# Attention with a causal mask on one core: the next head's maxima are dealt out over the steps by another table

## The reference

```
attn = jnp.einsum('bhqd,bhkd->bhqk', q, k) * SCALE
attn = jnp.where(causal[None, None], attn, -jnp.inf)
probs = jax.nn.softmax(attn, axis=-1)
out = jnp.einsum('bhqk,bhkd->bhqd', probs, v)
```

## Time and profile before

| | |
|---|---|
| median of three executions | 1719.4 us |
| the profiled execution | 1721.68 us |
| its span, first to last instruction | 1719.9 us |
| what lies outside the span | 1.8 us |
| granted TensorE clock, mean over the span | 0.988 of full |
| PE, DVE, ACT, POOL busy | 97%, 68%, 64%, 53% |

### The profile page before, as it was taken

How to read it: one execution, slowest core, us unless ns; L and a number is a source line. 1 busy time by engine, 2 the same in 40 slices (tenths; PEclk the granted TensorE clock), 3 DMA queues, 4 the chain that set the end, 5 groups by cost and what they waited for, 6 DMA issues and landing times.

```text
span 1719.9 us, 30467 instructions
## 1 busy us (share of the span) xinstructions
PE 1660.3 (97%) x9262; PEld 1369.7 (80%) x9262; DVE 1161.7 (68%) x2377; ACT 1104.9 (64%) x1684; POOL 906.1 (53%) x764
## 2 busy tenths in 40 slices
PE   7999999999999999999986999999999999999996
PEld 7987677767767776776665999999999999999992
DVE  6437777777777777778697676665665566556544
ACT  3222788787878887887686566666665565556544
POOL 2321888878788888882764433434334343343422
PEclk9999999999999999999997999999999999999998
DMA  7676211111111111112664897897987887788776
GB/s 241 188 220 196 62 50 50 49 49 49 49 49 49 49 49 49 49 49 74 232 229 128 287 269 225 245 274 208 281 237 201 224 265 217 208 249 239 192 190 217
DMA packets 103715, 276.87 MB, mean 161 GB/s; under 512 B 19833, under 2 KB 37625, under 8 KB 93625
## 3 DMA queue, kind: packets, MB, share of 16 engines
q1 hardware_dynamic: 78169, 213.29, 38.0%
q0 software_dynamic: 25440, 62.27, 17.4%
HBM read 194.75 MB, written 63.72 MB: 150 GB/s over the span
## 4 chain that ended last, share of the span: by engine, by line
PE 87%; DVE 6%; issue 2%; DMA 2%; ACT 2%; POOL 1%; SPq 0%; DVEq 0%; ACTq 0%; POOLq 0%
PE p_prj L91 26%; PE a_op L883 11%; PE a_mp L842 8%; PE a_sp L901 7%; PE p_at_ps L91 7%; PE p_logit_ps L91 7%; PE e_qp L91 5%; PE a_op L874 5%; PE p_ht_ps L2057 3%; PE e_vp L91 2%; PE p_at_ps L2080 2%; DVE part_max L759 2%; PE a_sp L905 1%; PE a_shared L860 1%; PE a_mp L845 1%
## 5 line engine op out<-in xcount | busy, mean ns | idle before, releaser
L709 POOL TENSOR_TENSOR prob_lo<-prob,prob_hi 128x1024 fp32r<-128x1024 f32 x211 | 451.5, 2157 | 141.6 <-DVE prob_hi L788 132.6
L759 DVE TENSOR_REDUCE part_max<-a_mp 128x1 f32<-128x512 f32 (+2 forms) x600 | 359.5, 610 | 70.5 <-PE a_mp L842 40.4
L1446 POOL DMA_INDIRECT acc_rows<-m_y_out,m_row_ids x108 | 176.1, 1631 | 410.7 <-ACT m_y_out L1615 385.9
L744 ACT ACTIVATE prob<-a_sp 128x1024 f32<-128x1024 f32 x320 | 293.6, 930 | 64.4 <-PE a_sp L905 34.9
L91 PE MATMUL p_prj<-m_w_hi,m_ht_hi 128*128 128x352 f32 x888 | 297.5, 335 | 1.8 <-DVE m_ht_lo L1855 1.4
L91 PE MATMUL p_prj<-m_w_lo,m_ht_hi 128*128 128x352 f32 x888 | 288.0, 324 | 0.0
L91 PE MATMUL p_prj<-m_w_hi,m_ht_lo 128*128 128x352 f32 x888 | 287.0, 323 | 0.0
L1879 DVE TENSOR_TENSOR m_w_lo<-m_w_raw,m_w_hi 128x704 fp32r<-128x704 f32 (+1 forms) x357 | 270.7, 797 | 22.8 <-ACT m_w_hi L1621 22.4
L1621 ACT ACTIVATE m_w_hi<-m_w_raw 128x704 fp32r<-128x704 f32 (+1 forms) x357 | 229.0, 713 | 17.5 <-PE p_prj L91 16.8
L1865 DVE TENSOR_TENSOR m_at_lo<-p_at_ps,m_at_hi 128x384 fp32r<-128x384 f32 x111 | 61.8, 557 | 252.0 <-ACT m_at_hi L1607 252.0
L731 ACT ACTIVATE prob_hi<-prob 128x1024 fp32r<-128x1024 f32 x216 | 203.2, 941 | 6.8
(11 more groups left out here) (314 smaller groups left out, 3336.0 us busy)
## 6 DMA issues: line engine op xcount, KB each, us to landing
m_w_raw<-wexp SPq DMA_DIRECT2D x51, 1408.0 KB
m_w_raw<-wexp SPq DMA_DIRECT2D x51, 768.0 KB
qk_parts<-rows SPq DMA_DIRECT2D x64, 256.0 KB, 3.2
multi<-qk_parts SPq DMA_DIRECT2D x42, 256.0 KB, 5.0
acc_rows<-p_zeros SPq DMA_DIRECT2D x2, 4352.0 KB, 18.8
v_head<-v_all SPq DMA_DIRECT2D x16, 520.0 KB, 3.0
k_stack<-qk_parts SPq DMA_DIRECT2D x21, 256.0 KB, 4.1
q_stack<-qk_parts SPq DMA_DIRECT2D x21, 256.0 KB, 6.2
```

The lines of the kernel that those rows point to most:

```text
L709: nc.gpsimd.tensor_tensor(prob_lo[:, t % RING, :, c0:NB], prob[:, t % RING, :, c0:NB], f32(prob_hi[:, t % RING, :, c0:NB]), ALU.subtract). ...
L744: nc.scalar.activation(prob[:, t % RING, :, c0:NB], sp_[:, t % 2, :, c0:NB], ACT.Exp, scale=SCALE).then_inc(prob_ready, 1)
L759: nc.vector.reduce_max(part_max[:, qb, kb:kb + 1], mp[:, n % 2, 0:width], AX_X).then_inc(piece_done, 1)
L1446: nc.gpsimd.indirect_dma_start(acc_dram[sum_of(t)], bass.IndirectOffsetOnAxis(ap=row_id(t), axis=0), y_out[:, t % 4, :], None, compute_op= ...
```

## The change

One table has other numbers, with the same sum of 40. No instruction is added or removed.

```
-PIECES_AT = (0, 0, 0, 0, 0, 3, 4, 3, 4, 2, 1, 2, 1, 3, 3, 3, 3, 3, 3, 2)
+PIECES_AT = (0, 0, 0, 0, 0, 3, 3, 3, 3, 3, 2, 3, 2, 3, 3, 3, 3, 2, 2, 2)
```

## The result

Over nine executions the changed kernel took 1726.65 us in the median (1724.26 to 1729.43), the kernel before, on the same chips, 1722.88 us (1718.43 to 1723.72). The ratio is 1.0029 with a 95% interval of 1.0019 to 1.0039: slower by 5.0 us (3.3 to 6.7); the two medians alone are 3.8 us apart. The forecast was +3.6 us. It was put as a median of 1723.0 us because the kernel before then had 1719.4 us from three executions; on the 1722.88 us of nine, the same +3.6 gives 1726.5. The interval lies around the bound of 0.3% set beforehand, so the runs say "slower", but not on which side of that bound.

What follows compares the result with a forecast made beforehand. PE, 97% busy, bounds the kernel; its waits for DVE cost 1.6 us per head. Terms -0.46 - 0.40 + 0.21 + 1.00 - 0.09 = +0.26 per head, +3.6 us over 14 heads: median 1723.0 us, range 1715 to 1729.

Steps and rivals of the forecast that it cites:

- Steps 6 and 8: PE no longer waits for piece 6 or back-to-back pieces 12 and 13: 0.46 and 0.40 us saved per head.
- Step 9: Three pieces between half-wide products: PE waits for piece 12's bank and restarts once, 0.21 us added per head.
- 10 to 12: Steps 10 to 12 get one piece more each, 0.24 us of PE work each, with nothing waiting.
- Step 13: Its first piece, 22, waits 0.90 us behind tile 10's subtraction, plus 0.10 restart: 1.00 us added per head; delay ends there.
- 14: Step 14: pieces 23 and 24 come late enough that step 13's delay ends before them; no stall added.
- 15: Step 15: piece 30 waits 0.34 us plus 0.10 restart, against 0.53 before: 0.09 us saved per head.
- 16 to 19: Steps 16 to 19 have two or three pieces with full products between; 0 us of stall change.
- The meeting of DVE and POOL: DVE asks for tile 10 with 0.81 us of POOL's tile 11 left, and pays 0.67 us.
- The slower rival: DVE stays late past step 13, so pieces 26, 28 and 30 wait: +0.56 us per head, 1727.2 us; chance 0.20.
- Only the gains come: Tile 10's subtraction gets ahead of POOL's tile 11 and takes 1.22 us: -0.4 per head, 1713.7 us; chance 0.12.
- the subtraction costs what it did: Tile 10's subtraction on DVE still takes 1.58 us: -0.05 us per head, 1718.7 us; chance 0.16.

Runs made afterwards that it cites:

- experiment 1: Steps 5 to 9 as in the change, later ones as in the kernel before, but step 10 has two pieces instead of one; 1715.03 us, ratio 0.9961 to before.
- experiment 5: Changed kernel, but in step 11 DVE takes tile 10's subtraction ahead of the third piece; 1722.68 us, ratio 1.0005 to the kernel before.
- experiment 6: Table of experiment 1 with one piece moved from step 9 to step 12; 1709.28 us, ratio 0.9931 to the kernel before.
- experiment 2: Steps 5 to 9 as in the kernel before, later ones as changed, but step 16 has two pieces instead of three; 1737.25 us, ratio 1.0090 to before.
- experiment 4: Changed kernel, but DVE instead of POOL makes prob_lo of tile 11, in step 12; 1771.67 us, ratio 1.0294 to the kernel before.
- experiment 3: Changed kernel, but POOL instead of DVE makes prob_lo of tile 10; 1716.39 us, ratio 0.9964 to the kernel before.

## Why the prediction was right, point by point

The forecast was +0.26 us per head; measured were +0.37. Step by step, from the lengths of the steps (from scores to scores, means over heads 2 to 13) less the work of the pieces moved:

| step | length before | now | piece work moved | stall added | forecast |
|---|---|---|---|---|---|
| 6 | 3.11 | 2.49 | -0.23 | -0.40 | -0.46 |
| 8 | 2.74 | 2.04 | -0.23 | -0.48 | -0.40 |
| 9 | 1.68 | 2.22 | +0.23 | +0.31 | +0.21 |
| 10 to 12 | 6.08 | 6.80 | +0.70 | +0.02 | 0 |
| 13 | 2.11 | 3.10 | +0.06 | +0.93 | +1.00 |
| 14 | 2.05 | 1.93 | -0.18 | +0.05 | 0 |
| 15 | 2.21 | 2.25 | +0.11 | -0.07 | -0.09 |
| 16 to 19 | 8.82 | 8.37 | -0.46 | +0.01 | 0 |

- *Steps 6 and 8*: right in kind; together -0.88 against -0.86, but so close by luck. Step 6 saved 0.06 less than forecast, mostly since the transposes start 0.11 behind the mask matmul and not 0.06, and step 8 saved 0.08 more.
- *Step 9*: the wait was right (1.18 for the bank), the restarts were not. I counted one; there are two, of 0.11 and 0.10 us. That is the largest error of size, and the 0.07 forecast too much for step 13 hides most of it.
- *The meeting of DVE and POOL*: right in kind and nearly in size. Step 11 of head 7 now begins at 472.00; DVE comes to tile 10 at 475.62 - 472.00 = 3.62 and POOL starts tile 9 at 472.41 - 472.00 = 0.41, both as forecast. POOL ends tile 11 at 4.38, not 4.43, so I had 0.81 us of tile 11 left and a price of 0.67 where it was 0.76 and 0.62. All of the runs lie on one line, price = rest of POOL's instruction - 0.13 or 0.14:

| kernel | POOL's rest when DVE comes | DVE pays |
|---|---|---|
| experiments 1 and 5 | 0.23 | 0.10 |
| before | 0.50 | 0.36 |
| experiment 6 | 0.70 | 0.56 |
| changed | 0.76 | 0.62 |
| experiment 2 | 0.89 | 0.76 |
| experiment 4, tile 11 | 2.23 | 2.09 |

  It is the same the other way round. Before, `rows` on POOL starts at 474.91, while DVE's subtraction has 476.03 - 474.91 = 1.12 us to go, and takes 1.38 instead of 0.39: it pays 0.99, the rest less 0.13. The Trainium skill ("SBUF — State Buffer", section "SBUF: two separate sides") has as a rule that, of a VectorE instruction with two SBUF inputs and a GpSimd instruction that reads SBUF, the one that starts first keeps the port pair that they share and the other stands until it is done. All seven kernels of this table agree with it to within 0.14 us. Where they differ the measurement decides: the changed kernel pays 0.62, not the full 0.76. What the constant of 0.13 to 0.14 is, no run here shows.
- *Step 13*: the wait was 0.84 (0.90 forecast) and the delay ended there: steps 14 to 19 add nothing (0.05 - 0.07 + 0.01). The slower rival, that DVE would not catch up, did not happen, though the measured time lies between my forecast and it. The 0.11 per head above the forecast are the 0.10 of step 9's second restart and small errors of both signs.
- *Only the gains come* needed 1.22 us for tile 10, and *the subtraction costs what it did* 1.58; both fall with the measured 1.84 us.
- Experiments 1, 3 and 5 take the meeting with tile 11 away in three ways (one piece fewer ahead of the subtraction, no subtraction, an earlier one), and each time step 13's wait goes. So it is shown, not argued, that the loss of 0.93 per head comes from tile 10 in DVE's queue. Its two parts are POOL and the place in the queue, and experiment 4 has the second without the first: same table, same place of tile 10, POOL idle. There the piece waits 0.22 us instead of 0.84. So POOL's share is 0.62, just what the subtraction is longer by, and the queue alone costs 0.22 of waiting and 0.10 for the restart.

## What to carry to other kernels

Evening out a table of fillers by their number per step is not the same as evening out the waits: a filler with a two-deep buffer has a period (here 1.18 us per two pieces), and a step must be long enough for it, so short steps want fewer. Look at what stands behind the last filler of a step on the engine that consumes them: one more filler there moves a long instruction, and with it the moment at which two engines meet. When instructions of two engines hold each other up, as the subtractions of DVE and POOL do here, where they start can matter more than how long they are: moving tile 11's subtraction from POOL (1.29 us) to DVE (0.69 us) made the kernel 3% slower, and putting tile 10's ahead of a reduction instead of behind it took 0.5 us off it and 0.3 us off each head.

## What the runs showed of the hardware that I had not expected

In experiment 4 PE idled from about 498.7 to 501.0 us in step 13, waiting for DVE. Its granted clock, 1.00 of full (2.4 GHz) from 488 to 498 us, was 0.53 on the mean from 501 to 508 us, so mostly at the lower level of 1.2 GHz, and 1.00 again from 508 us. These are rows of head 7, which took 45.69 us against 41.19 in the changed kernel: of the 4.5 us lost, 2.1 fell in step 13 (5.17 instead of 3.11), and 2.4 in steps 14 and 15 (3.52 and 3.02 instead of 1.93 and 2.24), where PE waited for nobody. So about half of this head's loss was not the wait but what followed it.

The same run shows that it is the clock. Step 13 took 4.9 to 5.2 us in all of heads 1 to 14, yet in heads 6, 10 and 13 the clock stayed at 1.00 throughout (427.70 to 470.80 us for head 6), steps 14 and 15 took 1.93 and 2.25, and the head 43.1 us. The other eleven, where it fell, took 44.3 to 45.7 us. In the other nine kernels, with waits of up to 0.91 us in step 13, the granted clock stayed at 1.00 from 300 to 770 us.
